# First-half gates in fp32, high halves of eight weight pieces on ScalarE, and new orders ahead of the groups

## The reference

```python
q, k = rope(bf16(x @ Wq.T)), rope(bf16(x @ Wk.T))
o = (where(causal, exp(q @ k.T / 16), 0)).sum(axis=-1)      # one number per row
x = layernorm(x + relu(o @ fc1_w.T + fc1_b) @ fc2_w.T + fc2_b)
xa = x @ P_w.T                                               # routing address, 64 numbers
C1, C2, C3 = (top3_softmax(xa @ U.T) for U in (U1, U2, U3))  # 12 weights a row, 3 not zero
h = gelu(sum_e C1[:, e] * (x @ W1[e].T))
y = sum_e C2[:, e] * (h @ W2[e].T) + C3 @ b2
out = layernorm(x + y)
```

## Time and profile before

| | us |
|---|---|
| median of 3 runs (lowest, highest) | 304.25 (303.53, 304.68) |
| the profiled execution | 303.71 |
| span of its profile | 301.9 |
| of it outside the span | 1.8 |
| TensorE busy | 259.2 (86%) |
| VectorE busy | 216.0 (72%) |
| GpSimd busy | 188.8 (63%) |
| ScalarE busy | 174.6 (58%) |

### The profile page before, as it was taken

One profiled execution on the slowest core, in us unless ns is written; L12 is line 12 of the kernel. 1 busy time (PEld: TensorE's weight loads), 2 busy tenths in 40 slices (PEclk: granted clock), 3 DMA queues, 4 the chain that ended last, 5 costly groups with the idle time before them and its releaser, 6 DMA issues.

```text
span 301.9 us, 6455 instructions
## 1 busy us (share of the span) xinstructions
PE 259.2 (86%) x2000; PEld 190.4 (63%) x2000; DVE 216.0 (72%) x668; ACT 174.6 (58%) x374; POOL 188.8 (63%) x381
## 2 busy tenths in 40 slices
PE   6999669995869688789599899899898998998960
PEld 4444334543334466568389789798797896887950
DVE  0369538989731795978689889899898787765661
ACT  1246742953266165542767875966968858554531
POOL 2620503999999899534778477575686764755532
PEclk9999897997979899989799999999999999999997
DMA  8996699991000000000001001010101010101101
GB/s 227 394 397 240 102 209 161 200 148 23 0 0 0 2 0 3 0 0 21 18 3 37 17 22 37 17 38 20 37 20 35 21 37 18 38 20 35 26 29 55
DMA packets 19466, 20.44 MB, mean 68 GB/s; under 512 B 1627, under 2 KB 18790, under 8 KB 18918
## 3 DMA queue, kind: packets, MB, share of 16 engines
q1 hardware_dynamic: 18438, 19.07, 26.7%
q10 hardware_dynamic: 992, 0.93, 1.1%
HBM read 15.71 MB, written 4.19 MB: 66 GB/s over the span
## 4 chain that ended last, share of the span: by engine, by line
PE 53%; POOL 23%; DVE 8%; ACT 6%; issue 6%; DMA 2%; POOLq 0%; SPq 0%; DVEq 0%; ACTq 0%
PE bank L1077 37%; PE bank L901 8%; POOL W L462 7%; POOL wtmp L459 5%; POOL W L461 4%; DVE early L1494 2%; DMA early<-in_xT 2%; PE bank L1159 2%; ACT early L715 1%; ACT early L823 1%; PE bank L1026 1%; POOL rstd L488 1%; PE bank L974 1%; PE bank L962 1%; DVE xturn L1247 1%
## 5 line engine op out<-in xcount | busy, mean ns | idle before, releaser
L1077 PE MATMUL bank<-W,x1T 128*128 (+1 forms) x630 | 76.3, 276 | 5.2 <-issue 3.2
L1077 PE MATMUL bank<-W,early 128*128 (+1 forms) x630 | 76.4, 276 | 3.6 <-DVE early L1494 1.4
L1077 PEld LDWEIGHTS bank<-W,x1T 128*128 128x128 f16 x630 | 60.9, 99 | 16.0 <-issue 5.9
L1077 PEld LDWEIGHTS bank<-W,early 128*128 128x128 f16 x630 | 61.7, 99 | 12.5 <-DVE early L1494 1.9
L901 PE MATMUL bank<-early,wqk 128*128 128x512 f32 x128 | 65.2, 646 | 1.3 <-DMA early<-in_xT 1.3
L1494 DVE SCALAR_TENSOR_TENSOR early<-bank,Csel,early 128x256 f32<-128x256 f32 x95 | 45.8, 482 | 17.3 <-PE bank L1077 8.8
L587 POOL TENSOR_TENSOR early<-early 128x256 f32<-128x256 f32 x29 | 21.0, 724 | 31.3 <-DVE early L1494 31.3
L901 PEld LDWEIGHTS bank<-early,wqk 128*128 128x128 f32 x128 | 24.6, 208 | 24.4 <-issue 23.6
L657 ACT ACTIVATE qk<-bank 128x512 bf16<-128x512 f32 x32 | 19.1, 596 | 33.3 <-PE bank L901 33.3
L1247 DVE TENSOR_TENSOR xturn<-qk,turn 128x2048 bf16<-128x2048 bf16 x16 | 20.5, 1284 | 21.6 <-ACT qk L657 21.6
L773 ACT ACTIVATE early<-early 128x256 f32<-128x256 f32 x32 | 13.3, 417 | 35.4 <-DVE early L1494 35.3
(11 more groups left out here) (134 smaller groups left out, 448.4 us busy)
## 6 DMA issues: line engine op xcount, KB each, us to landing
early<-in_xT SPq DMA_DIRECT2D x16, 256.0 KB, 7.5
xs<-in_x SPq DMA_DIRECT2D x32, 128.0 KB, 7.4
out<-early SPq DMA_DIRECT2D x32, 128.0 KB
W<-in_w1T SPq DMA_DIRECT2D x1, 2048.0 KB, 12.3
W<-in_w2T SPq DMA_DIRECT2D x1, 2048.0 KB, 12.9
W<-in_w1T SPq DMA_DIRECT2D x1, 1024.0 KB, 7.8
W<-in_w2T SPq DMA_DIRECT2D x1, 1024.0 KB, 14.6
wqk<-in_wqkT ACTq DMA_DIRECT2D x1, 512.0 KB, 3.8
```

The lines of the kernel that those rows point to most:

```text
L1077: mm = pe.matmul(where[:, 0:DIM], lhs(hx, c), w, start=(k == 0), stop=(k == 5))
```

## The change

- The gates of T = 0 and 1 no longer pass GpSimd. TensorE transposes the column of o of a sequence, read 32 times over, with four fp32 transposes for each half quarter (`gate_spread`); ScalarE applies weight, bias and relu in one instruction (`gate_relu`); `fc` of groups 0 to 3 multiplies in fp32 by a new fp32 copy of fc2 (`fc2w`, one more DMA, ahead of the twelve small ones). T = 2 and 3 keep the old way.
- For the W2 pieces GpSimd no longer casts; ScalarE makes the high half from the source (`w2_high`), and GpSimd waits for it ahead of the subtraction.
- C is written ahead of C3f in `weights_of`, and who needed C3f waits for it by a semaphore of its own.
- The order is changed in many places of all engines up to tile 4.

```diff
@@ sync @@
             load_chunk(3)
+            sp.dma_start(fc2w[:, :], fc2[0:2 * PAD, :]).then_inc(ld_fc2, 16)
             sp.wait_ge(fc2_split, 1)
@@ gpsimd @@
-                link(pool.tensor_copy(W[:, m, e + 1, 0, :], wtmp[:, n % 2, :]))
+                if m:
+                    pool.wait_ge(piece_high, n - (NE - NB) + 1)
+                else:
+                    link(pool.tensor_copy(W[:, m, e + 1, 0, :], wtmp[:, n % 2, :]))
                 pool.tensor_tensor(W[:, m, e + 1, 1, :], wtmp[:, n % 2, :], W[:, m, e + 1, 0, :], ALU.subtract)\
...
-                    early_aux(c, j, early)
-                    if (c, j) == (NCH - 1, 0):
-                        early_aux(c, 1, early)
-                        C3_split(0)
-                    if (c, j) in ((2, 3), (5, 0)):
-                        gate_parts(c // 4)
+                    if (c, j) == (3, 3):
+                        norm_scale(0)
+                    if (c, j) == (5, 1):
+                        norm_scale(1)
+                    if (c, j) == (6, 2):
+                        chosen_exps(0)
+                        weights_of(0)
                     if c >= 4:
                         w_piece(piece)
                         piece += 1
+                    if (c, j) == (NCH - 1, 0):
+                        C3_split(0)
...
             w_piece(piece)
-            norm_scale(2)
...
             bias_add(0, 0)
+            norm_scale(2)
             gate_parts(2)
@@ scalar @@
+            def gate_relu(c):
+                T, b = c // 2, SPC * (c % 2)
+                act.wait_ge(gate_done, c + 1)
+                act.activation(hgf[PAD * T:PAD * (T + 1), :, b:b + SPC, :].rearrange("p u s r -> p s u r"),
+                               bank[HGT][0:PAD, :].rearrange("p (s u r) -> p s u r", s=SPC, r=RPS), ACT.Relu,
+                               bias=gatew[0:PAD, 1:2], scale=gatew[0:PAD, 0:1]).then_inc(gate_copied, 1)
...
+            def w2_high(n):
+
+
+                act.wait_ge(w_split, NE - NB + n)
+                act.activation(W[:, 1, NB + n + 1, 0, :], Wf[:, WS + NB + n + 2, :], ACT.Copy, scale=scale[:, 2:3])\
+                    .then_inc(piece_high, 1)
...
                 early_aux(c, 0, early)
+                if c == NCH - 2:
+                    w2_high(0)
                 early_aux(c, 1, early)
+                if c == NCH - 1:
+                    w2_high(4)
...
+                if 1 <= c <= 4:
+                    gate_relu(c - 1)
+                if c == NCH - 2:
+                    w2_high(1)
+                if c == NCH - 1:
+                    w2_high(5)
...
+                if c == NCH - 2:
+                    w2_high(2)
+                    x1_high(1, 0)
+                    w_high(NB)
+                    w2_high(3)
+                if c == NCH - 1:
+                    w2_high(6)
+                    w_high(NB + 1)
@@ tensor @@
+            def gate_spread(c):
+                T, b = c // 2, SPC * (c % 2)
+                pe.wait_ge(exp_done, SPC * (c + 1))
+                wait(pe, gate_copied, c)
+                for s in range(SPC):
+                    tr = pe.transpose(bank[HGT][0:PAD, P * s:P * (s + 1)],
+                                      o[:, T, b + s:b + s + 1].to_broadcast([P, PAD]), identf[:, :])
+                tr.then_inc(gate_done, 1)
...
+                if (s, pos) == (3, 1) and group(k + 1):
+                    route_count(k + 1)
...
             C3_transpose(0)
+            routed_first(1)
             pe.wait_ge(exp_done, SPC * NCH)
             h_transpose(0)
             bias(0, 0)
-            routed_first(1)
@@ vector @@
                     if group(k + 1):
                         route_sums(k + 1)
+                        w_low(NB)
+                        route_ids(k + 1)
...
-                if c != 3:
-                    early_aux(c, 1, early)
+                early_aux(c, 1, early)
...
                 if c == NCH - 1:
+                    w_low(NB + 1)
                     break
...
-            route_ids(0)
-            first_mixture(0, (1,))
             rope(NCH - 1, 1)
-            first_mixture(0, (2, 3))
+            first_mixture(0, (1, 2, 3))
...
             route_ids(1)
+            norm_stats(3, (0,))
             second_mixture(1)
             fc_add(3, 1)
             row_stats(1)
             h_low(2)
             x1_low(2, 1)
+            norm_stats(3, (1,))
             first_mixture(3)
-            norm_stats(3)
             fc_add(4, 0)
```

More of the change, by code:

```diff
@@ L202, in build @@
         ld_rows = sem("ld_rows")
+        ld_fc2 = sem("ld_fc2")
+        gate_done = sem("gate_done")
+        gate_copied = sem("gate_copied")
         fc2_split = sem("fc2_split")
@@ L251, in build @@
         C_done = sem("C_done")
+        C3f_done = sem("C3f_done")
         csel_done = sem("csel_done")
@@ L468, in gate_parts @@
                 pool.wait_ge(exp_done, NSEQ * (T + 1))
-                wait(pool, hgT_done, T)
-                if T == 0:
+                wait(pool, hgT_done, T - 2)
+                if T == 2:
                     pool.wait_ge(gwb_done, 1)
@@ L533, in select_of @@
                 c.then_inc(csel_done, 1)
-            def early(k, s, pos):
-                if (s, pos) == (0, 1) and group(k + 2):
-                    norm_scale(k + 2)
-                if (s, pos) == (3, 0) and group(k + 1):
-                    chosen_exps(k + 1)
-                if (s, pos) == (3, 1) and group(k + 1):
-                    weights_of(k + 1)
             def aux(k, s, pos):
@@ L732, in early @@
                         normed(k + 2, 1)
-                if (s, pos) == (3, 0) and group(k + 2):
-                    x1_high(k + 2, 0)
+                if (s, pos) == (3, 0) and k == -2:
+                    x1_high(0, 0)
             def aux(k, s, pos):
@@ L739, in aux @@
                         C3T_copy(k)
+                if (k, s, pos) == (1, 0, 0):
+                    normed(3, 0)
+                    final(1)
                 if (s, pos) == (0, 1):
@@ L827, in _ @@
             begin(0)
-            w_high(NB)
+            w2_high(7)
+            w_high(NB + 2)
             exps(NCH - 1, 0)
-            w_high(NB + 1)
+            w_high(NB + 3)
             exps(NCH - 1, 1)
-            w_high(NB + 2)
             gelu(0)
             C3T_copy(0)
+            begin(1)
             h_high(0)
             bias_copy(0, 0)
-            begin(1)
             gelu(1)
             normed(2, 0)
-            w_high(NB + 3)
             bias_copy(0, 1)
@@ L853, in _ @@
             gelu(3)
-            normed(3, 0)
-            final(1)
             for i in range(GT, NT + 2):
@@ L917, in scores @@
                               start=False, stop=True, skip_group_check=True).then_inc(score_done, 1)
-            def gate_transpose(T):
-                pe.wait_ge(hgp_done, T + 1)
-                wait(pe, hgT_copied, T)
-                if T >= 2:
-                    pe.wait_ge(x1lo_done, begun["x1T"])
-                    wait(pe, C3T_copied, begun["C3T"])
+            def gate_spread(c):
[6 more added lines that the diff above has]
+                tr.then_inc(gate_done, 1)
+            def gate_transpose(T):
+                pe.wait_ge(hgp_done, T - 1)
+                wait(pe, hgT_copied, begun["gate"])
+                pe.wait_ge(x1lo_done, begun["x1T"])
+                wait(pe, C3T_copied, begun["C3T"])
                 begun["gate"] += 1
-                spread = bank[GATE[T]][0:NP * NI, :].bitcast(BF16)
+                spread = bank[XPOSE][0:NP * NI, :].bitcast(BF16)
                 for b in range(NSEQ):
@@ L953, in fc @@
                 if g == 0 and h == 0:
+                    pe.wait_ge(ld_fc2, 16)
+                if T == 2 and g % 2 == 0 and h == 0:
                     pe.wait_ge(fc2_spread, 16 * NP)
-                if h == 0:
-                    pe.wait_ge(hgT_copied, T + 1)
+                if h == 0 and T < 2:
+                    pe.wait_ge(gate_copied, 2 * (T + 1))
+                if h == 0 and T >= 2:
+                    pe.wait_ge(hgT_copied, T - 1)
                 wait(pe, bias_copied, begun["bias"])
@@ L1132, in _ @@
                 early_aux(c, 3, early)
+                if 1 <= c <= 4:
+                    gate_spread(c - 1)
             def first(js):
@@ L1390, in route_sums @@
                 dve.wait_ge(ezm_done, g + 1)
-                wait(dve, C_done, g)
+                wait(dve, C3f_done, g)
                 link(dve.tensor_reduce(esum[:, :, :].rearrange("p t r -> p (t r)"), ez[:, :, :], AX.X, ALU.add))
@@ L1555, in _ @@
             second_mixture(0, range(0, 3))
-            w_low(NB + 2)
             route_max(1)
-            second_mixture(0, range(3, 6))
-            w_low(NB + 3)
-            second_mixture(0, (6, 7))
+            second_mixture(0, range(3, 8))
             route_strike(1)
```

49 lines of the change are left out of this document (22 added, 27 removed).

## The result

The changed kernel takes 309.73 us (308.77 to 311.38, 4 runs) against 303.89 us (301.88 to 304.68, 4 runs) for the kernel before: ratio 1.021, interval 1.014 to 1.028. It is slower; 300.0 us was predicted, and the range ended at 304.8. The profiled execution took 311.38 us with a span of 309.6, which is 1.7 us above the median; positions in its trace are late by about that. The ratios leave out runs that lie more than 1.5% above the fastest of their kernel, while the medians take in all runs.

A forecast was written before the change was run, and what follows sets the result against it. The start of the regular loop was taken to decide, behind stretches held by GpSimd's weight pieces, VectorE's tile 0 slots, then TensorE. Loop 4.1 us earlier: 303.71 to 299.6 profiled, median 0.5 above, so 300.0 us; range 295.5 to 304.8.

The forecast's parts named there:

- rival 3: Slower through ScalarE: late W1 pieces delay chunk 7's copies and the low half ahead of the last rope; 306.6 us, chance 0.13.
- Start to the scales: From kernel start to GpSimd's first weight piece: scales ready at 51.8 instead of 52.56, about 0.8 us gained.
- at most 0.97: Bound on the new fp32 fc pair on TensorE, half of a projection's 1.94 us at full clock.
- The W1 pieces: GpSimd's first eight pieces, without the gate instructions: last one ends at 82.0 instead of 87.06, 5 us earlier.
- My bounds for such meetings: Each of the last three W1 pieces meets a VectorE rope or not: end at 79.9 with none, 84.7 with three.
- the point of 86.1: End of the last W1 piece at or behind which the slower rival decides.
- The handoffs: Chunks 6 and 7, called disputed: ScalarE's W2 high halves cost more than the pieces gained; last rope ends 108.0, not 105.0.
- Last rope to the statistics: VectorE's stretch behind the last rope: 8.2 us as now plus 0.5 for the first slot, statistics at 116.7.
- Second mixture: Tile 0's second mixture: low halves made earlier, heading 2.6 us gained and 2.2 left; ends at 129.0 instead of 131.5.
- To the loop: From tile 0 to the bias products: new order of group 3's statistics and C3T copy off the path, 1.7 us more gained.
- three additions: Parts of the slower rival: late W1 pieces 3.6 us, chunk 7's four products at 2.65 each 1.4, eight handoffs 1.6.
- The 0.2 us for each handoff: Extra cost the slower rival put on each of eight handoffs, 1.6 us together.

The follow-up runs named there:

- Version 3: Changed kernel with the second fc of group 0 behind chunk 3's last product and the first fc_add behind peak_pow: 305.22 us.
- version 2: Changed kernel with VectorE's first fc_add back behind the bound and the rope of chunk 3: 310.04 us.
- Version 9: Changed kernel with GpSimd casting the W2 pieces again, plus seven gate instructions of T = 1 back on GpSimd, result unused: 300.98 us.
- Version 11: Changed kernel with all eight handoffs kept but placed later, second fc behind chunk 3's last product, VectorE's second W2 low half behind the last rope: 297.85 us.
- edit 6: Changed kernel with VectorE's second low half of W2 moved behind the last rope, and on ScalarE w_high(NB + 2) behind chunk 7's first exps: 305.41 us.
- version 1: Changed kernel without handoffs: GpSimd casts the W2 pieces itself again, ScalarE makes none of their high halves: 297.82 us.
- Version 10: Changed kernel without handoffs, second fc behind chunk 3's last product, and GpSimd's weights of group 0 two pieces earlier: 295.13 us.
- version 5: Changed kernel without handoffs and with the second fc of group 0 behind the last product of chunk 3: 293.40 us.
- version 7: Changed kernel without handoffs, with the statistics of group 3 in one piece behind the slots of tile 3, as before the change: 300.86 us.

## Why the prediction was wrong

Up to the last rope the chain that I walked was the right one: both waits of TensorE for the handoffs stand where they were expected, GpSimd's free time turned into waits for ScalarE, and rival 3 named the copies of chunk 7 and the low half ahead of the last rope. Behind the rope I left out a wait. The sizes were wrong, all in one direction. From my stations to those of the changed trace:

| stretch | predicted us | measured us | error |
|---|---|---|---|
| first piece | 51.8 | 54.51 | +2.7 |
| first piece to end of the eighth | 30.2 | 31.7 | +1.5 |
| eighth piece to end of last rope | 26.0 | 27.2 | +1.2 |
| last rope to statistics | 8.7 | 11.7 | +3.0 |
| statistics to second mixture | 2.6 | 3.0 | +0.4 |
| second mixture | 9.7 | 9.8 | +0.1 |
| from there to the bias products | 15.5 | 17.5 | +2.0 |
| bias products | 144.5 | 155.43 | +10.9 |

**Start to the scales: 0.8 us gained.** This step failed; 1.95 were lost. The load came 1.2 us late: VectorE's add started at 43.17, not 42.0. Part of that is chance: the eight issues began 0.7 us later than before (32.67 for 31.98), where I had 0.43, and in the six versions that keep the changed order of chunk 3 on TensorE and VectorE this add started anywhere from 41.81 to 43.17. The fp32 `fc` took 2.07 us, where I had "at most 0.97" from a row at full clock. I had written that the wait ahead of it grows and kept the slow 3.48 for the product behind it, but not for the `fc` itself. The granted clock of 43.9 to 46.0 is 0.50, the lower of the two levels (1.2 GHz), after TensorE had stood still for 4.88 us:

```profile
43.90:46.00 2.10, 2.09 (x5) 1.25 (x6) 1.85 (x3) 0.00 (x0) 0.00 (x0) 0.50 1.19 296
```

The step also has a small slip of its own: the product that moves from 45.37 to 44.4 gives 1.0 us, not 0.8. Version 3 shows what stood behind the load: taking the wait off this path gives 3.8 us. VectorE's order (version 2) is not the cause.

**The W1 pieces: 5 us earlier.** Half right. From the first piece on they were 2.8 us shorter than before (31.7 against 34.5), not 4.3. I had costed the scale of group 1 at its busy time, but it waits 1.54 us for VectorE's statistics. Version 9 gives the same size from the other side, 2.9 us. The first four pieces took 13.85 us where 14.9 stood, the other four and the scale 17.9 where 15.3 stood. The Trainium skill, page "SBUF — State Buffer", section "Who interferes with whom", has GpSimd and a VectorE instruction with two SBUF inputs exclude each other for a whole instruction. The trace agrees in that equal subtractions again took 1.15 us or up to 2.23. My bounds for such meetings end at 84.7. The wait and the late start put it at 86.23, behind the point of 86.1 that I had set for rival 3. That point did not fit the rival's own price, which reaches 306.6 us with the eighth piece at 84.7.

**The handoffs.** 26.0 us predicted, 27.2 measured: the term that I called disputed was the best one. What was wrong was its weight. The same stretch takes 17.9 us before and 13.4 without the handoffs, so they cost 13.8 us against their own alternative. I set them against the old kernel alone, found it "bought nothing up to here", and looked for the gain elsewhere. The product behind the wait in chunk 7 took 3.62 us, not 2.65. Version 11 splits the cost of the handoffs: 7.4 us came from places (theirs and, with edit 6, that of VectorE's low half), and 4.4 stayed, now with 1.82 us of waiting for a copy in chunk 7 and 4.21 for ScalarE ahead of tile 0.

**Last rope to the statistics: the first slot on top, 0.5.** This step failed by 3.0. I added the slot's time to VectorE and left out who waits for it. The first mixture has four banks; with no slot added before the rope, TensorE fills them, stops (2.83 us, <-DVE early), and the remaining slots come at its pace. In version 1, where six of these products take 1.07 us and not 1.46, the stretch takes 10.6 us. Version 10 comes nearest to a test: with the same order behind the rope TensorE waits only 0.92 us, the six products take 0.83, and the stretch takes 9.0 us, where it takes 11.6 in version 5 with a wait of 3.09. So most of the 3.0 comes with the wait. How it divides between the time that TensorE stands still and the slower products behind it stays open, since in version 1 these products were not at full clock either.

**Second mixture.** Right: 9.8 for 9.7. The heading of that step has gains of 2.6 and 2.2 us, while its own positions, 131.5 and 129.0, give 2.5; the sum went by the positions.

**To the loop: 1.7 us gained.** Right in mechanism, hidden by the clock. From the route count of group 1 to the last bias products the changed kernel takes 15.54 us, before 15.21. But `second(1)` at 143.10 took 3.71 us against 2.14 in version 1, where the stretch is 13.97: the difference of 1.57 is exactly that. Without slow products the stretch is 1.2 us shorter than before, and version 7 without the order takes 17.3 (1.6 of that again slow products).

**Range and chances.** Rival 3 was priced at 306.6 with 0.13. Two of its three additions came: the pieces late, and the four products of chunk 7 with 10.8 us in all where it has 10.6. The 0.2 us for each handoff was not measured by itself. On top came the start and the slot. The large errors point one way because three of them share a part: in the changed kernel TensorE's products behind the new waits of 4.88, 3.74 and 2.83 us were slow, and I charged that only where the old trace already showed it. The stations sum to 10.9 us of error in the profiled execution, the loop adds 0.8 (it takes 153.3 us from its first product to the end of the span, 152.5 before); the median is 9.7 us above the forecast.

## What to carry to other kernels

Work handed to an engine with spare time can cost what stands behind it in that engine's queue, not its own 0.7 us: put it behind the instructions that third engines wait for, or leave it where it is. Price each edit against the version that has everything else but it, not only against the kernel before; here one bad edit hid a set of good ones. When a change adds an idle stretch to TensorE, price the products behind it at the low clock level as well.

## What the runs showed of the hardware

- The fp32 pair of `fc` (two products of 256 columns over 32 rows) took 1.12 us at full clock and 2.07 at a granted clock of 0.50; the bf16 pair takes 0.39. Half of a projection, 0.97, was not the bound that I took it for.
- Equal histories, unequal clock. In the changed kernel and in version 1 TensorE does the same 5.9 us of work with the same pauses, and the stretch with the next product has a granted clock of 0.55 in the one and 1.00 in the other. The windows of both, first the changed kernel:

```profile
137.20:143.10 5.90, 5.01 (x41) 3.60 (x38) 5.65 (x19) 3.94 (x6) 3.07 (x10) 1.00 0.00 1
143.10:146.80 3.70, 3.70 (x20) 2.79 (x20) 1.32 (x5) 0.22 (x1) 1.21 (x8) 0.55 0.15 40
```
```profile
125.30:131.20 5.90, 5.01 (x41) 3.60 (x38) 5.65 (x19) 3.94 (x6) 3.08 (x10) 1.00 0.00 0
131.20:133.80 2.60, 2.60 (x25) 2.41 (x25) 1.68 (x6) 0.42 (x2) 1.21 (x8) 1.00 0.20 57
```

  What lies further back differs, and no run here tells which part of it decides. For a kernel with such stretches it means a spread of 1.6 us at one place, 2.8 in version 5 with the fc pair, that no step of its own explains.
